# Ranks ahead of the weighing's second part, slots between two halves of the line terms, and a later load of x, in an attention and expert block on one core

## The reference, cut to what matters

```python
q = _plucker_lines(q1, q2); k = _plucker_lines(k1, k2)      # 16 heads, 6 components
# a component is p1[i] * p2[j] - p1[j] * p2[i], then lines / norm
logits = einsum('bhtc,bhsc->bhts', q, k @ _J6.T) * 6 ** -0.5   # causal
o = einsum('bhts,bhsd->bhtd', softmax(logits), v)
x = _layernorm(x + o @ Wo.T + bo)
scores, idx = top_k(sigmoid(x @ Wr.T + rb), 2)
x = _layernorm(x + shared(x) + sum over the two picks of score * expert(x))
```

## Time and profile before

| | us |
|---|---|
| median of 3 runs | 969.52 (966.25 to 973.77) |
| the profiled execution | 962.28 |
| its span, first to last instruction | 960.5 |
| TensorE busy in it | 734.7 (76%) |
| VectorE busy | 618.6 (64%) |
| GpSimd busy | 590.7 (61%) |
| ScalarE busy | 564.7 (59%) |

### The profile page before, as it was taken

One profiled execution on the slowest core, in us unless ns is written; L12 is line 12 of the kernel. 1 busy time (PEld: TensorE's weight loads), 2 busy tenths in 40 slices (PEclk: granted clock), 3 DMA queues, 4 the chain that ended last, 5 costly groups with the idle time before them and its releaser, 6 DMA issues.

```text
span 960.5 us, 22767 instructions
## 1 busy us (share of the span) xinstructions
PE 734.7 (76%) x7168; PEld 447.9 (47%) x7168; DVE 618.6 (64%) x1580; ACT 564.7 (59%) x875; POOL 590.7 (61%) x901
## 2 busy tenths in 40 slices
PE   2799997988988998898888777677766776758700
PEld 2444444434434444444443356565655555646600
DVE  7638888897788777977877367733333343333585
ACT  1488867667766867677777744334444454444436
POOL 3456667678768878778887744234454555444465
PEclk8599979899989989899999889988899898898855
DMA  6001011011201111120101622348332334221387
GB/s 225 12 24 28 19 52 48 30 59 47 66 22 49 60 38 50 44 66 28 58 26 45 190 65 70 78 74 217 84 70 62 74 68 79 67 55 32 91 228 209
DMA packets 125914, 69.85 MB, mean 73 GB/s; under 512 B 62820, under 2 KB 114278, under 8 KB 125840
## 3 DMA queue, kind: packets, MB, share of 16 engines
q1 hardware_dynamic: 106576, 43.44, 17.9%
q0 software_dynamic: 8512, 17.06, 5.7%
q10 hardware_dynamic: 10752, 8.39, 2.9%
HBM read 29.25 MB, written 31.21 MB: 63 GB/s over the span
## 4 chain that ended last, share of the span: by engine, by line
PE 40%; DVE 15%; issue 14%; ACT 10%; POOL 7%; another core or an unknown queue 6%; SPq 5%; DMA 2%; ACTq 0%; POOLq 0%; DVEq 0%
PE O L742 13%; PE S L727 8%; PE S L918 7%; ACT probs L1069 4%; PE O L940 4%; PE W L700 3%; POOL probs L554 3%; DVE hid L1617 3%; ACT hid L1198 2%; POOL prodB L542 2%; DVE prodA L1271 2%; SPq L452 2%; DVE hid L1599 1%; PE W L766 1%
## 5 line engine op out<-in xcount | busy, mean ns | idle before, releaser
L1069 ACT ACTIVATE probs<-S 128x1024 f32<-128x1024 f32 x320 | 319.7, 1043 | 149.5 <-PE S L727 125.5
L554 POOL TENSOR_SCALAR_AFFINE_SELECT probs<-probs 128x256 f32<-128x256 f32 (+1 forms) x448 | 218.1, 517 | 123.3 <-ACT probs L1069 122.7
L633 POOL DMA_INDIRECT z_scratch<-y,tails x136 | 133.9, 985 | 156.5 <-ACT y L1171 124.3
L742 PE MATMUL O<-probs,v_aug 128*32 128x512 f32 (+3 forms) x2048 | 187.5, 489 | 21.7 <-POOL probs L554 21.7
L1617 DVE TENSOR_TENSOR hid<-hid 128x512 f16<-128x512 f32 x100 | 70.6, 706 | 183.8 <-ACT hid L1198 157.3
L1179 ACT ACTIVATE silu<-S 128x512 f32<-128x512 f32 x100 | 59.9, 599 | 181.1 <-PE S L918 97.8
L940 PE MATMUL O<-w_T,hid 128*128 (+1 forms) x1200 | 102.4, 237 | 83.6 <-DVE hid L1617 67.8
L267 POOL DMA_INDIRECT rows_scratch<-xrow,slot_i x128 | 132.4, 1034 | 47.5 <-issue 29.6
L727 PE MATMUL S<-qkT 32*128 32x512 f16 (+3 forms) x1024 | 139.9, 317 | 20.0 <-ACT probs L1069 9.1
L940 PEld LDWEIGHTS O<-w_T,hid 128*128 128x128 f16 x1200 | 84.1, 106 | 105.6 <-issue 86.0
L918 PE MATMUL S<-xT_rt,w_T 128*128 128x256 f16 (+1 forms) x864 | 117.8, 289 | 7.8 <-issue 4.5
(11 more groups left out here) (155 smaller groups left out, 989.6 us busy)
## 6 DMA issues: line engine op xcount, KB each, us to landing
z<-z_scratch SPq DMA_DIRECT2D x32, 256.0 KB, 4.2
xT<-in_x_cols ACTq DMA_DIRECT2D x16, 256.0 KB, 2.8
x_in<-in_L_attn_x ACTq DMA_DIRECT2D x16, 256.0 KB
x_scratch<-x SPq DMA_DIRECT2D x16, 256.0 KB, 2.6
x1T_scratch<-x1T SPq DMA_DIRECT2D x16, 256.0 KB
xT_sh<-x1T_scratch SPq DMA_DIRECT2D x16, 256.0 KB
x_in<-x_scratch SPq DMA_DIRECT2D x16, 256.0 KB
out<-res SPq DMA_DIRECT2D x16, 256.0 KB, 4.2
```

The source lines that it names most:

```text
L554: pool.affine_select(out=v, in_=v, compare_op=ALU.is_ge, fill=0.0, base=0, pattern=[[0, v.shape[1]], [1, P]], channel_multiplier=-1).then_ ...
L633: pool.indirect_dma_start(out=z_dram, in_=y[:, q, a, :], in_offset=None, out_offset=bass.IndirectOffsetOnAxis(ap=tails[:, q, a, 1:2].bitca ...
L742: mm = pe.matmul(O[g // 2][32 * j:32 * j + 32, kb * P:T], value_weights(par, kb, g, j), probs[:, g % 2, c, col:col + T - kb * P], start=(g ...
L1069: act.activation(probs[:, g % 2, c, :], S[(g + c) % 2][:, :], ACT.Exp, scale=-SCALE / SPLIT_UP ** 2).then_inc(s_exp, 1)
```

## The change: what it does

TensorE issues `ranks(b - 3)` between `logits(0, 3)` and the second part of `weigh(b - 1, ..., 3)` and no longer behind `logits(0, 4)`. VectorE issues three of the six line terms, then `slots(b - 3)`, then the other three. ScalarE issues the load of x of batch b + 2 ahead of the exps of group 1 and no longer ahead of those of group 0; the load of the columns stays.

```diff
@@ TensorE, body @@
                 if not first:
                     weigh(b - 1, 1 - par, 3, (0,))
                 logits(0, 3)
+                if sends(b):
+                    ranks(b - 3)
                 if not first:
                     weigh(b - 1, 1 - par, 3, (1, 2, 3))
                 logits(0, 4)
-                if sends(b):
-                    ranks(b - 3)
@@ ScalarE, body @@
                 if ahead(b):
                     load_columns(b + 2, par)
-                    load_x(b + 2, par)
                 exps(b, 0, (0,))
...
                 if not last:
                     copy_values(b + 1, 1 - par)
+                if ahead(b):
+                    load_x(b + 2, par)
                 exps(b, 1, range(NCHUNK))
@@ VectorE @@
-            def line_terms(c):
-
-                dve.wait_ge(pts_read, 2 * (c + 1))
-                for dst, many, one in products(prodA, 1, 0):
-                    ins = dve.tensor_tensor(dst, many, one, ALU.mult)
-                chain(ins)
+            def line_terms(c, part=None):
+
+                if part != 1:
+                    dve.wait_ge(pts_read, 2 * (c + 1))
+                for k, (dst, many, one) in enumerate(products(prodA, 1, 0)):
+                    if part is None or k // 3 == part:
+                        ins = dve.tensor_tensor(dst, many, one, ALU.mult)
+                if part != 0:
+                    chain(ins)
@@ VectorE, body @@
                 if not last:
-                    line_terms(b + 1)
+                    line_terms(b + 1, 0)
                 if sends(b):
                     slots(b - 3, 1 - par)
+                if not last:
+                    line_terms(b + 1, 1)
```

## The result

The changed kernel takes **988.14 us** (median of 4 runs, 987.26 to 988.95); the kernel before, on the same chip, took 969.86 (4 runs, 966.25 to 973.77). The ratio is 1.0188, with an interval of 1.0147 to 1.0228: slower, where faster was forecast. The profiled execution took 988.95 us around a span of 987.2.

What follows compares the result with a forecast made beforehand. TensorE was taken to wait for VectorE's late slots() and GpSimd's masks. Held batches gave 9.0 us and batches 3 and 4 gave 1.4, so 962.28 - 10.4 = 951.9 us, rounded to 952; range 938 to 966.

Steps and rivals of the forecast that it cites:

- Ranks ahead: Five small TensorE matmuls moved before the weighing's second part: VectorE reads ranks 2.0 us earlier in batch 8, no cost.
- L766's wait goes: TensorE's transposes of the attention output: waits for VectorE shrink from 17.5 us to under 7, left in batches 3 and 4.
- Batches 3 and 4, -1.4 us: Batches that also prepare weights: slots() moves ahead of three products, 0.7 us each; bounds 0 and 7.3 us.
- The load, 0: ScalarE's issue of the load of x, 0.39 us, moved behind the first exps: costs nothing, gains 0.
- `slots()` at 1.7 us: VectorE: slots() taken at its batch 8 length, 299.93 to 301.65, so part 1 begins at 299.6.
- Part 1 was bounded on both sides: VectorE's last three line terms beside GpSimd's products: 0.7 us free, 5.21 held; costed at nothing between.
- rival C: VectorE's part 1 behind slots() held over 5.5 us, normalise() over 3.3 late, in every batch: 983 us; chance 0.09.
- Held batches get batch 8's length, -9.0 us: Batches 5, 7 and 11, at 34.42, 35.17 and 35.17 us, each fall to 31.93: 9.0 us saved.
- The cover behind it: VectorE 3.0 us late if part 1 is held; TensorE notices only after 3.3 us at L805, leaving 0.3.
- Rival A: VectorE held in part 1, GpSimd's masks end up to 1.6 us sooner, TensorE waits less: 938 us; chance 0.14.
- B: Wait paid back: holds in part 1 overshoot their cover or batches fall to a lower clock: 962 us; chance 0.20.
- The rule on the port: VectorE and GpSimd share an SBUF port pair by an exclusive lock per instruction: about 0.5 us a product, 1.5 in all.

Runs made afterwards that it cites:

- e12: The kernel before, unchanged, measured again for a second trace: 872.66 us with two runs, against 882.69 with 23, ratio 0.9896.
- e3: The kernel before with only the load of x moved, ranks and line terms as before: 965.03 us, ratio 0.9994.
- e4: The whole change, but the sum that slots() multiplies lies in PSUM, not SBUF: 963.12 us, ratio 0.9947 to the kernel before.
- e6: The whole change with slots()'s multiplied sum and its sum over experts in PSUM, cast from there, next_slot updated last: 964.71 us, ratio 1.0044 to the kernel before.
- e7: The whole change, with GpSimd's six products waiting until slots() is done: 970.75 us, ratio 1.0084 to the kernel before.
- e9: The kernel before with only the line terms split around slots(), ranks and loads where they were: 901.24 us, ratio 1.0214.
- e5: The whole change once more, for a second trace: 977.52 us, ratio 1.0175 to the kernel before.
- e13: The kernel before with the line terms split and one small PSUM-to-PSUM copy ahead of slots()'s products: 970.61 and 986.27 us, no ratio.
- e14: The kernel before with the line terms split and three small PSUM-to-PSUM copies ahead of slots()'s products: 979.74 us, ratio 1.0186.
- e16: The whole change a third time, on the third chip: 973.16 us, ratio 1.01 to the kernel before.

## Why the prediction was wrong, point by point

- **Ranks ahead: right, and worth little.** L1418 waits 6.3 us in eleven waits, 0.6 at most, and reads the ranks 4.9 us behind the first exp in batch 8, against 6.4. TensorE does not wait for the picks in the loop's batches; its two waits for them (1.4 us) lie behind the first exp of batch 15, and one of 1.1 was there before.
- **L766's wait goes: right.** As forecast it is left in batches 3 and 4 alone, with 3.2 us of the 7.3.
- **Batches 3 and 4, -1.4 us: right in sign, too small.** 33.74 and 34.66 against 35.19 and 36.68, together 3.5. Batch 4's part of it is not shown to be the change's: the kernel before took 34.89 there in e12, where L1405 was not held.
- **The load, 0: right** (e3). Batch 0's first exp starts 4.4 us sooner (27.2 against 31.6) and batch 1 at 64.04 against 64.21, so the gain of it is nothing.
- **`slots()` at 1.7 us: the step that failed.** Part 1 was bounded on both sides, with the 5.21 us of the earlier trace rows as the held end. The same bound was not laid on `slots()`, though the text, in rival C, says that it has "two more operations with two inputs under GpSimd's stream". 1.7 us was read from one batch, in which the two products ran in the middle of GpSimd's own and took 0.84; the prediction took that for their length at another place under the same stream. There they took 5.29 and `slots()` 6.1 us (298.20 to 304.33). No row of the kernel before showed that length for these products, but the earlier trace rows showed three products of the same kind both free and held, so the held case had to be priced for `slots()` too.
- **Held batches get batch 8's length, -9.0 us: wrong by that.** Batches 5 to 14 were forecast at 31.9 and took 34.76 in the mean. The three holds of the kernel before (line terms) became nine.
- **The cover behind it: named, and used up.** The prediction gave VectorE 3.3 us before TensorE notices at L805. `normalise()` came 3.7 later, and L805 waits 12.0 us in twelve waits. 0.4 past the cover is what the waits cost by the start of L805, 0.5 us; what makes 2.6 of it are the two levels of the clock (L805 and L779 together took 3.11 us and not 1.78).
- **Rival A's shorter wait for the masks came** (6.7 us and not 21.7), and was lost again on VectorE's side; B's waits for L805 and its clock came too, in more than six batches.
- **Rival C was the nearest** (983, for 988.95 in the profiled run): its kind, its threshold of 3.3 us and its engine were right, its place was not. In batch 8 part 1 ran in 0.74 us; e4 and e6, which take the products of `slots()` out of the hold, show it in part 1. That the number came near is in part luck: 13.1 of the 26.7 us lie behind batch 15's first exp, which C doesn't speak of. Its argument against itself, that 5.21 was the longest hold of three terms, was a weak one: how long a hold lasts depends on where GpSimd's stream is, and not on what is held.
- **The rule on the port.** The trace and the runs show which operations are held: two SBUF inputs 5.223 us, one of them in PSUM 0.189 (e4); a cast from SBUF to SBUF 4.67, from PSUM 0.17 (e6); GpSimd made to wait, 0.435 at most (e7). By the Trainium skill, page "SBUF — State Buffer", section "SBUF: two separate sides", VectorE and GpSimd share a port pair by an exclusive lock for a whole instruction; as to who is held, the runs agree. They do not agree with the length that follows if each instruction of GpSimd gave the lock back: then a product would wait for one instruction, about 0.5 us, and not for twelve. (The free batches do look like that: 0.37 and 0.55 us in batch 8 before.) The prediction took the length from that sum to dismiss the rule, while a row beside it (5.21) spoke for the longer hold.

What was shown: that the split is enough to make the loss (e9), that the products' operands in SBUF (e4) and GpSimd's stream (e7) are both needed for the hold in them, that taking `slots()` out of the hold takes most of the loss away (e4, e6 beside e5), and that the full holds end at the same place for three different starts, at the stream's first pause or one mask ahead (e9, e13, e14). Not the cause: a pause of VectorE, which is there without a hold (batch 8 before) and is missing with one (e16, batch 5). Open: what decides between a free batch, two short holds and a long one; whether the load adds to it; and, for the change itself, which share of the 18.3 us lies behind the start of batch 15.

## What to carry to other kernels

When an instruction is moved, ask not only what it waits for but what it will run beside: its duration belongs to its old neighbours. A VectorE instruction of two SBUF inputs, or a cast from SBUF to SBUF, under an unbroken stream of GpSimd is to be bounded by its own time and by the rest of that stream, until its first pause, however small it is: both ends occurred here at the same start. An operand in PSUM takes it out, but then a later one can be held, so look down the list. And a bound laid on one instruction of a kind is to be laid on all of that kind that the change touches.

## What the runs showed of the hardware that was not expected

- A product of 32 numbers a partition took 0.184 us alone and 5.223 under twelve GpSimd instructions; a cast of eight numbers 4.67.
- The end of a full hold does not move with its start: 9.9 or 10.6 us behind the first exp for starts of 6.6, 6.7 and 6.9 (e9, e13, e14).
- Two holds of 2.1 us in place of one of 5.2 came in exactly the batches in which an earlier product of VectorE had taken 1.1 us beside GpSimd's masks (15 batches of 15, and 0 of 42).
- The two products of one pair come in few forms: 5.2 and 0.18 or 0.44, 2.1 and 2.1, or free with 0.57 and 0.55 us (e16).
- The kernel before had medians of 960.8 to 969.9 us in four comparisons and 882.7 in one, on another chip, where the stretch behind batch 15 took 362 to 366 us and not 438 to 452.
- TensorE waited for its own matmuls, 14.4 us in twelve waits of up to 1.5 (L727 behind L727, above). The cause of that wait is open.
